# Expert blocks that gather, add and write back their output rows instead of adding into scratch rows with the DMA

## The reference

```
x = x + xattn(layernorm(x), ctx, mask)            # 16 heads, 77 keys
u = layernorm(x)
h = u + layernorm(u, ln1) @ attn_w.T
t = layernorm(h, ln2)                             # T = 2048 rows
top_vals, top_idx = top_k(t @ gate_w.T, 2);  rw = softmax(top_vals)
out = 0
for e in range(8):
    g, v = t @ gate_proj[e].T, t @ up_proj[e].T   # 256 -> 1024
    out += comb[:, e] * ((silu(g) * v) @ down_proj[e].T)
return x + h + out
```

## Time and profile before

| what | value |
|---|---|
| median of 3 runs | 651.98 us (651.53 to 652.48) |
| span of the profiled execution, first to last instruction | 645.5 us |
| its own time outside the span | not listed; the median less the span is 6.5 us |
| PE busy | 533.9 us, 83% of the span |
| DVE, ACT, POOL busy | 378.3, 250.4, 336.8 us |
| mean granted PE clock | 0.926 of full speed |

### The profile page before, as it was taken

One profiled execution on the slowest core, in us unless ns is written; L12 is line 12 of the kernel. 1 busy time (PEld: TensorE's weight loads), 2 busy tenths in 40 slices (PEclk: granted clock), 3 DMA queues, 4 the chain that ended last, 5 costly groups with the idle time before them and its releaser, 6 DMA issues.

```text
span 645.5 us, 13457 instructions
## 1 busy us (share of the span) xinstructions
PE 533.9 (83%) x3197; PEld 454.1 (70%) x3198; DVE 378.3 (59%) x896; ACT 250.4 (39%) x492; POOL 336.8 (52%) x422
## 2 busy tenths in 40 slices
PE   3489988889996515999999299999999999999770
PEld 2268877777775304888888188878878888788660
DVE  1846889999996473644334656474474434836430
ACT  1155756555553242433233252352343333425120
POOL 5346567767675465653343527466355533654320
PEclk9789999999998556899999699999999999999895
DMA  7950000000010005271121154507207211030113
GB/s 213 277 225 2 33 18 26 25 25 25 16 34 26 25 17 180 61 233 29 25 33 24 27 184 122 138 21 201 54 6 224 47 25 24 8 49 9 16 19 140
DMA packets 27090, 46.58 MB, mean 72 GB/s; under 512 B 9719, under 2 KB 22545, under 8 KB 26769
## 3 DMA queue, kind: packets, MB, share of 16 engines
q1 hardware_dynamic: 15312, 35.77, 16.7%
q0 software_dynamic: 9088, 9.52, 9.0%
q10 hardware_dynamic: 2656, 0.91, 0.7%
HBM read 36.67 MB, written 11.61 MB: 75 GB/s over the span
## 4 chain that ended last, share of the span: by engine, by line
PE 49%; DVE 25%; issue 11%; POOL 4%; DVEq 3%; DMA 3%; ACT 2%; POOLq 0%; SPq 0%; ACTq 0%
PE psum L1160 13%; PE psum L1162 13%; PE psum L1161 13%; PE psum L1190 4%; DVE split_w L949 3%; DVE picked L834 3%; DVE s_sb L796 3%; DVEq L355 2%; DVE stats L703 2%; DVE tb_hi L995 2%; PE psum L1040 2%; POOL rstd L487 2%; DMA wk<-in_wkT 1%; POOL s_sb L521 1%; PE psum L1199 1%
## 5 line engine op out<-in xcount | busy, mean ns | idle before, releaser
L1160 PE MATMUL psum<-split_w,tb_hi 128*128 x288 | 120.1, 417 | 25.6 <-DVE split_w L949 16.7
L1161 PE MATMUL psum<-split_w,tb_hi 128*128 x288 | 115.3, 400 | 0.0
L1162 PE MATMUL psum<-split_w,tb_lo 128*128 x288 | 115.3, 400 | 0.0
L1160 PE MATMUL psum<-split_w,aT_hi 128*128 x288 | 84.4, 293 | 1.3 <-DVE aT_lo L985 1.2
L1160 PEld LDWEIGHTS psum<-split_w,tb_hi 128*128 128x128 f32 x288 | 55.7, 193 | 37.9 <-issue 27.8
L1161 PE MATMUL psum<-split_w,aT_hi 128*128 x288 | 81.5, 283 | 0.0
L1162 PE MATMUL psum<-split_w,aT_lo 128*128 x288 | 81.4, 283 | 0.0
L571 POOL DMA_INDIRECT acc_rows<-o_sb,add_at x36 | 60.3, 1674 | 33.8 <-POOL add_at L569 33.8
L370 POOL TENSOR_TENSOR split_w<-w_raw,split_w (+1 forms) x8 | 46.5, 5816 | 59.1 <-DVE split_w L955 59.1
L985 DVE TENSOR_TENSOR aT_lo<-psum,aT_hi 128x512 fp32r<-128x512 f32 x72 | 46.4, 686 | 49.0 <-ACT aT_hi L678 49.0
L971 DVE TENSOR_SCALAR o_sb<-psum,blk 128x256 f32<-128x256 f32 x36 | 17.4, 484 | 96.5 <-issue 84.3
(11 more groups left out here) (158 smaller groups left out, 1077.9 us busy)
## 6 DMA issues: line engine op xcount, KB each, us to landing
w_raw<-in_experts SPq DMA_DIRECT2D x24, 768.0 KB, 4.5
w_raw<-in_experts SPq DMA_DIRECT2D x2, 3072.0 KB, 13.8
x_sb<-in_x SPq DMA_DIRECT2D x8, 256.0 KB, 5.2
z_rows<-rows SPq DMA_DIRECT2D x16, 128.0 KB, 1.7
acc_rows<-x_sb SPq DMA_DIRECT2D x16, 128.0 KB, 2.6
ceil_f<-in_mask ACTq DMA_DIRECT2D x2, 308.0 KB, 11.1
blk<-lists POOLq DMA_DIRECT2D x36, 1.0 KB
rows<-z_rows,gather_at POOLq DMA_INDIRECT x36, 4.0
```

Of the source, the lines that this page charges most:

```text
L1160: nc.tensor.matmul(dst, hi, w_hi, start=first, stop=False)
L1161: nc.tensor.matmul(dst, hi, w_lo, start=False, stop=False)
L1162: return nc.tensor.matmul(dst, lo, w_hi, start=False, stop=last)
```

## The change

`acc_rows` is gone. Phase 1 stores `x + h` straight into the output, and the token numbers in the lists become row numbers of the output (batch first). In phase 2 POOL, in the turn of block *s* (one turn before the block's results are written), gathers the output's present rows into a new buffer `so_far`; DVE's weighting becomes multiply by the weight *and* add `so_far`; and POOL writes the sum back with a plain indirect DMA. Rows of the lists' padding lie outside the output and are left out by both DMAs. The copy at the end is gone.

A row of the output may be touched by two experts, so a gather must come after the write of every earlier expert's blocks. A new table, `earlier_tab`, holds for each block 16 x (number of blocks of earlier experts, at least 1), and POOL waits for `added` to reach it before it issues the gather.

```
-            for b in range(BATCH):
-                sp.dma_start(out_tiles[:, b], acc_tiles[:, b]).then_inc(out_done, 16)
-            sp.wait_ge(out_done, 16 * BATCH)
+            sp.sem_inc(out_done, 1)
...
                 if has(c):
-                    pool.wait_ge(y_done, number(c) + 1)
-                    wait_count(pool, added, 16 * number(c))
+
+                    wait_apart(pool, y_done, number(c) + 1, pool_met)
+                    nc.gpsimd.indirect_dma_start(
+                        out_rows, bass.IndirectOffsetOnAxis(ap=add_at[:, c.par, :], axis=0),
+                        y[:, c.par, :], None, bounds_check=TOKENS - 1, oob_is_err=False).then_inc(added, 16)
+                if has(s):
+
+                    wait_count(pool, added, 16 * (number(s) - 1))
                     pool.sem_inc(pool_met, 1)
-                    nc.gpsimd.tensor_copy(add_at[:, c.par, :], blk[:, number(c), 0:1]).then_inc(add_at_done, 1)
-                    wait_apart(pool, add_at_done, number(c) + 1, pool_met)
+                    nc.gpsimd.tensor_copy(add_at[:, s.par, :], blk[:, number(s), 0:1]).then_inc(add_at_done, 1)
+                    if not isinstance(number(s), int) or number(s) > 0:
+                        earlier = entry(pool, earlier_tab, s, 16, 16 * BLOCKS)
+                        pool.wait_ge(added, earlier)
+                        pool.sem_inc(pool_met, 1)
+                    wait_apart(pool, add_at_done, number(s) + 1, pool_met)
                     nc.gpsimd.indirect_dma_start(
-                        acc_rows, bass.IndirectOffsetOnAxis(ap=add_at[:, c.par, :], axis=0),
-                        y[:, c.par, :], None, bounds_check=TOKENS + P - 1, compute_op=ALU.add).then_inc(added, 16)
+                        so_far[:, s.par, :], None, out_rows,
+                        bass.IndirectOffsetOnAxis(ap=add_at[:, s.par, :], axis=0),
+                        bounds_check=TOKENS - 1, oob_is_err=False).then_inc(read[s.par], 16)
...
+                 nc.vector.tensor_scalar(earlier_tab[:, :], b_of[:, :], 1.0, 16.0, ALU.max, ALU.mult))
...
                         wait_count(dve, added, 16 * (number(d) - 1))
-                        nc.vector.tensor_scalar(y[:, d.par, :], bank[7][:, 0:D], blk[:, number(d), 1:2].bitcast(F32), None, ALU.mult).then_inc(y_done, 1)
+                        dve.wait_ge(read[d.par], 16 * (number(d) // 2 + 1) if isinstance(number(d), int) else 16 * (2 * d[0] + d[1] // 2 + 1))
+                        nc.vector.scalar_tensor_tensor(y[:, d.par, :], bank[7][:, 0:D], blk[:, number(d), 1:2].bitcast(F32),
+                                                       so_far[:, d.par, :], ALU.mult, ALU.add).then_inc(y_done, 1)
```

More of the change, by code:

```diff
@@ L149, in xattn_moe @@
         z2_rows = nc.dram_tensor("z2_rows", (TOKENS + P, D), F32).ap()
-        acc_rows = nc.dram_tensor("acc_rows", (TOKENS + P, D), F32).ap()
+        out_rows = out.rearrange("b s d -> (b s) d")
         v_rows = nc.dram_tensor("v_rows", (SCORES, BATCH * VW), F32).ap()
@@ L235, in xattn_moe @@
         added_tab = sb("added_tab", [1, 1], I32)
+        earlier_tab = sb("earlier_tab", [1, J], I32)
         w_raw = sb("w_raw", [P, 2 * WCOLS])
@@ L247, in xattn_moe @@
         y = o_sb
+        so_far = sb("so_far", [P, 2, D])
         tiles_only = ExitStack()
@@ L326, in xattn_moe @@
         at_done, add_at_done, out_done = sem("at_done"), sem("add_at_done"), sem("out_done")
+        read = [sem(f"read{i}") for i in range(2)]
         x_tiles = x.rearrange("b (i p) d -> p i b d", p=P)
-        out_tiles = out.rearrange("b (i p) d -> i b p d", p=P)
-        z2_tiles = z2_rows[0:TOKENS, :].rearrange("(n b p) d -> n b p d", b=2, p=P)
-        acc_tiles = acc_rows[0:TOKENS, :].rearrange("(n b p) d -> n b p d", b=2, p=P)
+        out_tiles = out.rearrange("b (n p) d -> n b p d", p=P)
+        z2_tiles = z2_rows[0:TOKENS, :].rearrange("(b n p) d -> n b p d", b=2, p=P)
         x_sb_pairs = x_sb[:, :, :].rearrange("p (i b) d -> p i b d", b=2)
@@ L406, in _ @@
             sp.dma_start(z2_rows[TOKENS:TOKENS + P, :], zeros[:, :]).then_inc(pad_out, 16)
-            sp.dma_start(acc_rows[TOKENS:TOKENS + P, :], zeros[:, :]).then_inc(pad_out, 16)
             sp.wait_ge(v_in, 32)
@@ L417, in store @@
                 sp.wait_ge(acc_done, number(t) + 1)
-                sp.dma_start(acc_tiles[t[0], t[1]], of(x_sb, t)).then_inc(acc_out, 16)
+                sp.dma_start(out_tiles[t[0], t[1]], of(x_sb, t)).then_inc(acc_out, 16)
             pipeline(sp, store, TILES, 0, 0)
@@ L466, in _ @@
             nc.gpsimd.iota(fill[:, :, 0], pattern=[[1, LIST_COLS]], base=0, channel_multiplier=LIST_COLS).then_inc(iota_done, 1)
-            nc.gpsimd.iota(tokens[:, :, :], pattern=[[P, TILES], [0, TOPK]], base=0, channel_multiplier=1).then_inc(iota_done, 1)
+            nc.gpsimd.iota(tokens[:, :, :], pattern=[[P, TILES // BATCH], [SEQ, BATCH], [0, TOPK]], base=0, channel_multiplier=1).then_inc(iota_done, 1)
             nc.gpsimd.memset(fill[:, :, 1], 0).then_inc(iota_done, 1)
@@ L538, in _ @@
                 pool.wait_ge(z2_out[par], 16 * TILES // 2)
-            pool.wait_ge(pad_out, 32)
+            pool.wait_ge(pad_out, 16)
             pool.wait_ge(acc_out, 16 * TILES)
@@ L931, in _ @@
                  nc.vector.tensor_scalar(present_tab[:, :], steps[:, :], cum[:, EXPERTS - 1:EXPERTS], None, ALU.is_lt),
-                 nc.vector.tensor_scalar(added_tab[:, :], cum[:, EXPERTS - 1:EXPERTS], float(USUAL_BLOCKS), 16.0, ALU.max, ALU.mult))
+                 nc.vector.tensor_scalar(added_tab[:, :], cum[:, EXPERTS - 1:EXPERTS], float(USUAL_BLOCKS), 16.0, ALU.max, ALU.mult),
+                 nc.vector.tensor_scalar(earlier_tab[:, :], b_of[:, :], 1.0, 16.0, ALU.max, ALU.mult))
             step(nc.vector.tensor_scalar(wait_tab[:, :], e_of[:, :], 1.0, float(PARTS), ALU.add, ALU.mult),
```

## The result

The changed kernel takes 677.61 us (median of 4, 675.99 to 680.12) against 651.75 us before; the ratio is 1.0411, 95% interval [1.0392, 1.043]. It is slower by 26 us. The forecast was 672, in a range of 656 to 686.

The account below looks back on a forecast made before the run. It took PE to bound phase 2, with the all-DMA copy behind it; stalls 25.6 + clock 8.5 - end 14.3 = +19.8 us on the 645.5 span, plus 6.5 to the median, gave 672 us, range 656 to 686.

Parts of the forecast that it names:

- The five blocks named: First blocks 0, 11, 15, 20, 28: weighting waits for `so_far`, stalling PE's next down product; losses 3.1 to 6.3 us each.
- the chain from POOL's token gather to the weighting: At first blocks, write, landing, gather, landing: 8.6 us beside a weight load, 6.1 alone; bounds 5.4 and 13.5.
- the rival in which both DMAs wait behind the load: At blocks 11, 15 and 20 write and gather queue behind weight loading: chain 11.5 us, total 685 us; chance 0.11.
- the rival in which nothing stretches: Landings don't lengthen under the weight load: chains 6.1 us (block 0 shorter), total 661 us; chance 0.15.
- Signs that missed: DVE idle on `so_far` 4 to 8 us at five first blocks, elsewhere none except the last; PE idle 3 to 6.
- The pieces of the chain: Beside a load: write landing 4.1, POOL seeing it 0.2, gather landing 4.2, DVE 0.1 us; alone, landings 3.0 and 2.8.
- The chain of 4.9: First-block chain from the skill's constant, an estimated 2.3 us per 128 KB DMA; would give some 656 us.
- Stalls and clock: Five first-block stalls sum to 25.6 us; slowed PE clock afterwards adds 5 x 1.7 = 8.5 us, bounds 5.1 to 11.
- Block 28: First block with no weights left to load: chain 6.1 us, PE loses 3.7 us.
- Blocks 10 and 33: PE's two waits for split weights at expert changes: nothing added, 0 us.
- The end: Removing the final copy saves 13.0 us and the last write lands 1.3 us earlier: -14.3 us, -12.5 to -15.5.
- The base: Profiled span 645.5 us plus the 6.5 us between it and the median of 651.98, added to the forecast.

Follow-up runs that it names:

- Experiment 1: Kernel before, but the addition inside the indirect DMA goes straight into the output: no gather of output rows, no copy at the end; 643.48 us, ratio 0.9902.
- experiment 2: Changed kernel with POOL's turn reordered: write of the block before first, then weight split, gather of output rows, list, token gather; 654.40 us, ratio 1.0071.
- experiment 5: Changed kernel with both write and gather of output rows ahead of the weight split in POOL's turn; 647.04 us, ratio 0.994.
- experiment 4: Changed kernel where every block's gather, not only an expert's first, waits for the write of the block before it to land; 681.26 us, ratio 1.0479.
- experiment 3: Changed kernel gathering the router's rows, which nobody writes in phase 2, without the wait for earlier experts' writes; 665.50 us, ratio 1.0245.
- experiment 7: The kernel before, unchanged, profiled a second time; span 649.5, time 651.12 us.
- experiment 6: Kernel before with the addition inside the DMA straight into the output, no gather or copy, timed again; 642.48 us, ratio 0.9868.

## Why the prediction was right, and where its terms were off

**The mechanism and its places: right.** The five blocks named were the five that stalled, PE was held where the prediction said (`aT_lo` behind the waiting weighting), and PE stalled at no block that is not behind a first one. For block 15 the chain from POOL's token gather to the weighting was 459.45 - 451.08 = 8.4 us, forecast 8.6; the chains of blocks 11 and 20 took 8.5. No chain came near the 11.5 us of the rival in which both DMAs wait behind the load; and the write's landings below, longer beside the load than without it, speak against the rival in which nothing stretches. Experiment 1 takes the chain out and all stalls go; experiments 2 and 5 keep all work and waits and move them in POOL's queue, and most, then all, of the stalls go; experiment 4 adds waits, and in phase 2 nothing happens. So it is the chain's place behind split and token gather that costs.

**Signs that missed.** DVE waited for `so_far` not at five or six blocks but at twelve: also at the block behind each of the five and at block 32, where PE was not held up, and at the last, which was weighted 1.2 us later behind the last product than before (forecast under 1). The idle time of DVE reached 9.3 to 9.5 us at blocks 11, 15 and 20 (forecast up to 8), and PE's at block 1 was 2.26 (forecast 3 or more).

**The pieces of the chain: off in both directions.** From issuing the write to issuing the gather 4.95 us passed at block 15 (forecast 4.3), and that gather took 2.9 us to land (forecast 4.2). Only the trace of experiment 4 records when the writes landed (source view of the write's line, min, median, max from issue to landing):

```profile
L567 POOL DMA_INDIRECT out_x<-o_sb,add_at x36: 1020/1037/1042, 282.9 to 673.0; - x36
...
DMA to landing us min/median/max: 2.2/2.5/4.5
```

Beside the weight load, before the gathers of blocks 11, 15 and 20, they took 3.7 us (forecast 4.1), before that of block 28, with no load, 2.4 (forecast 3.0). But the gather was issued 1.0 us behind the landing, where the sum has 0.2, and in the changed kernel the write began 0.3 us behind the token gather, where it has nothing. That the chain came out at 8.4 to 8.5 us for 8.6 is luck: transfers put too long and POOL's own time put too short cancel. Of the gathers of output rows in the changed kernel (source view of that line) the median is the shortest landing of the token gather in the earlier trace rows:

```profile
L580 POOL DMA_INDIRECT so_far<-out_x,add_at x36: 1025/1035/1057, 277.8 to 665.3; - x36
...
DMA to landing us min/median/max: 2.3/2.8/4.9
```

The Trainium skill's 2.0 us plus the bytes ("DMA: Bandwidth & Descriptors", Anatomy of one DMA), an estimated 2.3 for 128 KB, is the shortest of these, and near the 2.4 of the write at block 28. The chain of 4.9 made of it was too short even there, where it took 6.7 us: POOL's and DVE's time around the two transfers is not in it.

**Stalls and clock: 34.7 us, forecast 25.6 + 8.5 = 34.1.** Block 28 was under-sized (4.5 for 3.7: its chain took 6.7 us for 6.1, from write to gather's issue 3.4 for 3.2, and the write stood 0.3 behind the token gather), block 0 over-sized (2.6 for 3.1: its gather landed in 3.5 us for 4.2). The clock cost 1.5 to 2.2 us a stall, the shortest of 2.3 us among them.

**Blocks 10 and 33: forecast 0, measured 1.0 and 0.7.** Experiments 1, 2 and 3 have neither, experiment 4 has both. PE's waits there are as long as before, so the forecast of no wait held; the time went by the slower clock behind them. Why it rose later there was not tried by itself.

**The end: forecast -14.3, measured -9.7, the step that failed.** I took the copy's 13.0 us as beside nothing. POOL's drain lay beneath it, out of sight in a chain that ended with the copy. After the change it shows; first SP's semaphore behind its wait for the last landing, then the drain:

```profile
L439 SPq EVENT_SEMAPHORE  x1: 17/17/17, 672.5 to 672.5; - x1
...
L140 POOLq DRAIN  x1: 3902/3902/3902, 671.8 to 671.8; - x1
```

The drain runs from 671.8 to 675.7, and the span ends at 676.0. The prediction had said that the span would end within 1 us of the last write's landing; it ended 3.5 us behind it. The other 1.1 us of the 4.6 lie ahead of the landing: the last weighting was some 0.5 us later than forecast, and the last write was issued 0.9 us behind it, where the sum has 0.1.

**The base: wrong by 4.8 us.** I put the 6.5 us between the span and the median outside the span. In every later run the time is 1.6 to 1.7 us above the span, so the profiled execution took about 647.1 us, 4.8 under its median, by a short phase 1 (experiment 7). Adding a sum on the span to the median was right only because the sum concerns phase 2 and the end.

Put together, from the forecast's 671.8: +4.6 for the end, +0.6 for the stalls, +1.7 for blocks 10 and 33, +3.4 for the late start of block 0 and -4.8 for the base make 677.3; measured 677.6. That the end and the base nearly cancel is luck.

## What to carry to other kernels

When a change adds a read behind a write, price it from where its instructions come free in their queue, not from the transfer: the same two waits cost 34 us behind a weight split, and some 5 us ahead of it, where they held up the split instead. A copy at the end covers whatever else closes the program, so its own length is the most that removing it can give. And before a span is compared with a median, know how far the profiled execution lies from it.

## What the runs showed of the hardware that was not expected

- POOL's queue ends with a drain after its last DMA: 6.2 to 6.5 us where the last DMAs add into DRAM (the kernel before in both profiles, experiments 1 and 6), 3.8 to 3.9 where they write plainly (the changed kernel, experiments 2 to 5). Why it is that long was not tried.
- Issuing an indirect DMA of 128 rows of 1 KB from POOL in phase 2 took 1.02 to 1.30 us for plain writes and gathers and 1.56 to 1.73 for adding ones. All 56 that were issued while DVE's two-operand pass over 2048 elements was already running took longer: 2.0 to 2.8 us, the adding ones 3.3 (the earlier trace rows are such places too). The 15 that began shortly before such a pass did not (1.03 to 1.24). These are counts over all nine traces; no run moved the pass by itself.
- The granted clock was 0.50 to 0.67 in the 4.7 us behind every stall of 2.0 us and more that the down products had (the changed kernel, experiments 2 to 4), and stayed at 1.00 behind the three of 1.64 to 1.67 us in experiment 2.
- Behind one and the same wait of 12.9 to 13.1 us before block 10 the granted clock in the next 4.6 us was between 0.50 and 0.68 in eight traces, 0.54 and 0.50 in the two of the kernel before. So a step of 1 us in one trace at such a place can be the clock alone.
